# Cross-attention block on one core: the column sum of the context folded to 64 rows and taken in one product

## What is computed

```
g_x     = (g_w     @ x_2 + g_b).T          # 1024 x 256
theta_x = (theta_w @ x   + theta_b).T      # 1024 x 256
phi_x   =  phi_w   @ x_2 + phi_b           # 256 x 1024
W   = theta_x @ phi_x / 1024
y   = (W @ g_x).T                          # 256 x 1024
wy  = w_w @ y + w_b
out = bn_gamma * (wy - bn_mean) * rsqrt(bn_var + 1e-5) + bn_beta + x
```

## Time and profile before

| | |
|---|---|
| median of 3 runs | 783.51 us (783.49 to 783.71) |
| profiled execution, its own time | 783.43 us |
| its span, first to last instruction | 781.6 us |
| PE busy | 773.8 us (99% of the span) |
| POOL, DVE, ACT busy | 526.5, 495.3, 304.3 us |
| chain that ended last | PE 98%, DMA 1% |

### The profile page before, as it was taken

The page is one execution under the profiler, slowest core; times in us unless marked ns, Lnnn a source line. Parts: engine busy times, 40 slices in busy tenths (PEclk is TensorE's granted clock), DMA queues, the critical chain, the costliest instruction groups (busy, mean ns, idle before and its releaser), DMA issues.

```text
span 781.6 us, 11639 instructions
## 1 busy us (share of the span) xinstructions
PE 773.8 (99%) x4066; PEld 668.8 (86%) x4066; DVE 495.3 (63%) x891; ACT 304.3 (39%) x514; POOL 526.5 (67%) x358
## 2 busy tenths in 40 slices
PE   7999999999999999999999999999999999999998
PEld 6688888888888888888888888888888888888887
DVE  3874865749657385664848657396574847658255
ACT  5534533414344243543425345143542325334231
POOL 5939995757858477785758857478685767847500
DMA  9815573370835508264280734608365181740202
GB/s 278 202 67 130 194 188 135 79 245 1 215 107 110 212 22 216 84 161 161 54 252 17 188 134 90 232 0 215 107 132 190 33 229 59 173 150 1 108 1 107
DMA packets 55415, 103.17 MB, mean 132 GB/s; under 512 B 2506, under 2 KB 38244, under 8 KB 55396
## 3 DMA queue, kind: packets, MB, share of 16 engines
q1 hardware_dynamic: 53264, 101.86, 44.6%
q10 hardware_dynamic: 2132, 1.05, 0.6%
HBM read 69.35 MB, written 33.55 MB: 132 GB/s over the span
## 4 chain that ended last, share of the span: by engine, by line
PE 98%; DMA 1%; POOL 0%; DVE 0%; ACTq 0%; ACT 0%; issue 0%
PE wbank L699 58%; PE gbank L699 38%; PE wbank L871 1%; PE wbank L745 1%; DMA ctx_sb<-in_ctx_dram 1%; PE wbank L723 0%; PE wbank L751 0%; POOL ctxT_lo L303 0%; PE wbank L735 0%; DVE ctxT L504 0%; ACT ctxT_hi L357 0%; ACTq L368 0%; DVE x_sb L676 0%; ACTq L142 0%; PE wbank L710 0%
## 5 line engine op out<-in xcount | busy, mean ns | idle before, releaser
L303 POOL TENSOR_TENSOR ctxT_lo<-ctxT,ctxT_hi 128x512 fp32r<-128x512 f32 x124 | 168.0, 1356 | 202.9 <-ACT ctxT_hi L357 202.9
L314 POOL TENSOR_TENSOR ctx_sum<-ctx_sum,ctxT 128x512 f32<-128x512 f32 x108 | 157.8, 1461 | 0.2
L332 POOL TENSOR_TENSOR x_lo<-x_sb,x_hi 128x1024 fp32r<-128x1024 f32 x60 | 142.4, 2410 | 0.0
L357 ACT ACTIVATE mt<-wbank 128x512 fp32r<-128x512 f32 x64 | 37.9, 598 | 230.6 <-PE wbank L699 230.6
L689 DVE SCALAR_TENSOR_TENSOR x_sb<-wbank,const,x_sb 128x512 f32<-128x512 f32 x110 | 77.5, 746 | 69.4 <-PE wbank L699 69.3
L699 PE MATMUL wbank<-ctxT_lo,ctxT_hi 128*128 128x512 f32 x512 | 120.2, 390 | 0.5 <-POOL ctxT_lo L303 0.5
L357 ACT ACTIVATE ctxT_hi<-ctxT 128x512 fp32r<-128x512 f32 x124 | 76.6, 629 | 91.3 <-DVE ctxT L504 91.0
L534 DVE TENSOR_TENSOR stage<-gbank,mt 128x384 f32<-128x384 f32 x64 | 28.3, 485 | 131.7 <-PE gbank L699 131.7
L699 PEld LDWEIGHTS wbank<-ctxT_lo,ctxT_hi 128*128 128x128 f32 x512 | 94.6, 188 | 19.0 <-POOL ctxT_lo L303 0.7
L504 DVE STREAM_TRANSPOSE ctxT<-ctx_sb 128x512 f32<-128x512 f32 x124 | 78.8, 683 | 10.4 <-DMA ctx_sb<-in_ctx_dram 10.3
L699 PEld LDWEIGHTS gbank<-ctxT_hi 128*128 128x128 f32 x512 | 78.9, 189 | 4.0 <-issue 2.3
(11 more groups left out here) (113 smaller groups left out, 1334.4 us busy)
## 6 DMA issues: line engine op xcount, KB each, us to landing
x_sb<-in_x_dram SPq DMA_DIRECT2D x16, 2048.0 KB, 7.7
out_dram<-x_sb SPq DMA_DIRECT2D x63, 512.0 KB, 2.8
ctx_sb<-in_ctx_dram SPq DMA_DIRECT2D x60, 512.0 KB, 8.5
ctx_sb<-in_ctx_dram SPq DMA_DIRECT2D x4, 256.0 KB, 6.2
ctx_sb<-in_ctx_dram ACTq DMA_DIRECT2D x4, 256.0 KB, 7.0
x_sb<-in_L_xattn_w_w_dram SPq DMA_DIRECT2D x1, 512.0 KB, 9.0
stage<-in_L_xattn_theta_w_dram SPq DMA_DIRECT2D x1, 512.0 KB, 14.4
phi_nat<-in_L_xattn_phi_w_dram SPq DMA_DIRECT2D x1, 512.0 KB, 13.5
```

Of the source, the lines that this page charges most:

```text
L303: nc.gpsimd.tensor_tensor(ctxT_lo[:, c, :], turned_ctx(b, c), f(ctxT_hi[:, c, :]), ALU.subtract).then_inc(sem_, 1)
L314: nc.gpsimd.tensor_tensor(ctx_sum[:, :], ctx_sum[:, :], src, ALU.add).then_inc(ctxT_used, 1)
L332: nc.gpsimd.tensor_tensor(x_lo[:, k, :], x_sb[par][:, k, :], f(x_hi[:, k, :]), ALU.subtract).then_inc(x_lo_made, 1)
L357: nc.scalar.activation(dst, src, ACT.Copy).then_inc(sem_, 1)
```

## The change

The 128 rows of `ctx_sum` are folded to 64 before the split. ACT copies rows 64 to 127 to `fold` (`move_sum`); POOL adds them to rows 0 to 63, once rounded into `sum_parts` and once in full precision into `ctx_sum`, and subtracts the one from the other into `fold` (`sum_rest`); ACT rounds that into rows 64 to 127 of `sum_parts` (`pack_sum`). PE takes one product of ones with `sum_parts`. The rounded copy of the last add goes. The order on the engines changes too: on POOL `sum_rest` comes after `prep_x`; on ACT `move_sum` comes after `prep_x` and `pack_sum` at the start of the batch, ahead of the rows of M (in batch 0: after theta); in batch 0 on PE `column_sums` comes after two of the four blocks of t.

```diff
                 else:
                     pool.wait_ge(ctxT_used, CH * b + c)
-                    if c == CH - 1:
-                        nc.gpsimd.tensor_tensor(sum_hi[:, :], ctx_sum[:, :], src, ALU.add).then_inc(sum_split, 1)
                     nc.gpsimd.tensor_tensor(ctx_sum[:, :], ctx_sum[:, :], src, ALU.add).then_inc(ctxT_used, 1)
 
             def sum_rest(b):
                 pool.wait_ge(ctxT_used, CH * b + CH)
-                pool.wait_ge(sum_split, 2 * b + 1)
-                nc.gpsimd.tensor_tensor(sum_lo[:, :], ctx_sum[:, :], f(sum_hi[:, :]), ALU.subtract).then_inc(sum_split, 1)
+                pool.wait_ge(sum_moved, b + 1)
+                up = slice(0, P // 2)
+                nc.gpsimd.tensor_tensor(sum_parts[up, :], ctx_sum[up, :], fold[up, :], ALU.add).then_inc(sum_split, 1)
+                nc.gpsimd.tensor_tensor(ctx_sum[up, :], ctx_sum[up, :], fold[up, :], ALU.add).then_inc(sum_split, 1)
+                pool.wait_ge(sum_split, 3 * b + 2)
+                nc.gpsimd.tensor_tensor(fold[up, :], ctx_sum[up, :], f(sum_parts[up, :]),
+                                        ALU.subtract).then_inc(sum_split, 1)
 
             def prep_ctx(b):
-                pool.wait_ge(sum_split, 2 * b)
+                pool.wait_ge(sum_split, 3 * b)
...
-                sum_rest(b)
...
             def body(b, half, par, nxt, nxt2):
                 if nxt:
                     prep_ctx(b + 1)
                     prep_x(b + 1, 1 - par)
+                    sum_rest(b + 1)
...
+            def move_sum(b):
+                act.wait_ge(ctxT_used, CH * b + CH)
+                nc.scalar.activation(fold[0:P // 2, :], ctx_sum[P // 2:P, :], ACT.Copy).then_inc(sum_moved, 1)
+
+            def pack_sum(b):
+                act.wait_ge(sum_split, 3 * b + 3)
+                hi(sum_parts[P // 2:P, :], fold[0:P // 2, :], sum_packed)
...
                 if not first(b):
+                    pack_sum(b)
                     m_rows()
...
                 if nxt:
                     prep_x(b + 1, half + (1 if par else 0), 1 - par)
+                    move_sum(b + 1)
...
                 def column_sums():
-                    pe.wait_ge(sum_split, 2 * b + 2)
-                    mm(S_BANK[:, :], ones_r[:, :], sum_hi[:, :], True, False)
-                    mm(S_BANK[:, :], ones_r[:, :], sum_lo[:, :], False, True).then_inc(s_done, 1)
+                    pe.wait_ge(sum_packed, b + 1)
+                    mm(S_BANK[:, :], ones_r[:, :], sum_parts[:, :], True, True).then_inc(s_done, 1)
...
                 theta(0, (2, 3))
-                if first(b):
-                    pe.wait_ge(zb_taken, 1)
-                    column_sums()
                 pe.wait_ge(gram_lo_made, 3 * b + 3)
                 pe.wait_ge(low_lo_made, 2 * b + 1)
                 t_block(0)
                 t_block(1)
+                if first(b):
+                    pe.wait_ge(zb_taken, 1)
+                    column_sums()
```

More of the change, by code:

```diff
@@ L101, in xattn_kernel @@
         ctx_sum = sb("ctx_sum", [P, C])
-        sum_hi = sb("sum_hi", [P, C], F32R)
-        sum_lo = sb("sum_lo", [P, C], F32R)
+        fold = sb("fold", [P, C])
+        sum_parts = sb("sum_parts", [P, C], F32R)
         ident = sb("ident", [P, P])
@@ L196, in xattn_kernel @@
         ctxT_used = sem("ctxT_used")
-        sum_split = sem("sum_split")
+        sum_moved, sum_split, sum_packed = sem("sum_moved"), sem("sum_split"), sem("sum_packed")
         x_hi_made, x_lo_made = sem("x_hi_made"), sem("x_lo_made")
@@ L339, in _ @@
                 sum_up(0, c)
-            sum_rest(0)
             for k in (2, 3):
@@ L344, in _ @@
                                         ALU.subtract).then_inc(first_x_lo_pool, 1)
+            sum_rest(0)
             def body(b, half, par, nxt, nxt2):
@@ L421, in _ @@
                 z_hi_part(j)
+            move_sum(0)
             def body(b, half, par, nxt, nxt2):
@@ L461, in body @@
                 theta(0)
-                if not first(b):
+                if first(b):
+                    pack_sum(b)
+                else:
                     next_hi(4)
```

## The result

The changed kernel takes **792.1 us** (median of 5, 791.03 to 792.3), the kernel before in the same comparison 783.71 us: a ratio of 1.0105, 95% interval 1.009 to 1.012. It is slower, 8.4 us by the medians; the forecast was 791.2 with a range of 787.9 to 793.2. The profiled execution took 792.1 us, its span is 790.1 us against 781.6.

The account below looks back on a forecast made before the run. PE was taken to bound the kernel (98% of the last chain). Terms -3.4 + 0.3 + 9.4 + 1.4 = +7.7 on 783.43 gave 791.1, plus 0.08 for the median: 791.2 us, range 787.9 to 793.2.

Parts of the forecast that it names:

- The removed product: PE, batches 1 to 15: one 128x512 product fewer per batch, 15 x 0.227 = -3.4 us.
- POOL's fold in ordinary batches, hidden: Batches 2 to 15: three 64-row operations at 1.30 us; ACT's pack ends 1.2 us before M's first row, no cost.
- The rival at half the price: POOL's 64-row operations take half the time: 789.2 us, or 787.8 without the clock term; chance 0.12.
- The fourth row of M: Last three transposes wait for M's fourth row from ACT: 0.02 x 15 = +0.3 us, bounds 0 and 3.4.
- the handoff of 0.12: Time from ACT's finished fourth row of M to PE's weight load, 0.12 us, used to size that wait.
- Batch 0: Sum product moved behind two blocks of t; the fourth block, waiting for the bank, starts near 46.0: net +0.2 us.
- Batch 1's pause: ACT's wait for POOL's late fold holds the rows of M; PE idles some 9 us: +9.4 us, once.
- The clock: After batch 1's pause PE runs some products at the low clock: +1.4 us, bounds 0 and 2.8.
- The rival on the other side: No pause of PE in batch 1: -2.9 us, 780.6 us, faster than before; chance 0.06.

Follow-up runs that it names:

- experiment 4: Kernel before the change without the sum product of the low part, nothing added or moved; 780.19 us, ratio 0.9954.
- experiment 6: Changed kernel; from batch 1 on ACT packs after the high parts of S, PE takes the sum product behind the low bank's transposes; 783.61 us.
- experiment 3: Changed kernel with 32 products of 128x512 into an unused bank in PE's pause of batch 1; 789.94 us.
- experiment 1: Changed kernel with POOL folding batch 1's sum before the four x_lo instead of after them; 787.56 us, ratio 1.0036.
- experiment 2: Changed kernel with ACT packing the sum after the rows of M in batch 1 only; 788.22 us, ratio 1.0065.
- experiment 5: experiment 1 plus one wait: in batch 1 POOL begins the next context after DVE's three gram_lo; 781.31 us, ratio 0.9973.
- experiment 9: experiment 5 plus batch 1's pack between M's first two rows; in batch 0 pack before theta, sum product after one block of t; 780.68 us.

## Why the prediction was right

- **The removed product**: -3.4 forecast; the period fell by 0.219 us in 14 batches, and experiment 4 gave 3.5 us for 16. Right.
- **POOL's fold in ordinary batches, hidden**: forecast with 1.2 us of cover, measured 1.36. The price of a 64-row operation, taken at 1.30 between bounds of 0.65 and 1.64, is 1.25 to 1.30 where nothing else disturbs it: half the rows cost the same as all of them (1.28 for 128x512). The trace agrees with what the prediction took from the Trainium skill's GPSIMD Engine Reference (section 2, Architecture). The rival at half the price falls.
- **The fourth row of M**: forecast +0.3, measured at most 0.1 (14 times 0.227 less 0.219). In an ordinary batch the ten transposes take 1.06 us from their start to the next product (422.42 to 423.48), and 1.07 in the kernel before (412.49 to 413.56), so that the rows show no such wait with one product left. The step that was mis-sized is the handoff of 0.12 from the earlier trace rows; in experiment 6 it is 0.05. The mechanism is there, and decides as soon as the last product is moved too.
- **Batch 0**: forecast +0.2. PE's fourth block of t starts at 46.02, 0.22 after 45.80, but that agreement is luck: 0.18 was there before the first change of order (the last pair of theta stands at 40.76, before at 40.58, since the program's first load came later). From that pair to the fourth block it is 5.26 us against 5.22, so the change itself cost 0.04. The wait on the first block is there, but 0.26 us long (due at 45.76) where the forecast had 0.4.
- **Batch 1's pause**: forecast third part of M at 86.6, 9.4 later with the 0.2 of batch 0; measured 86.69, 9.3 us later than before. POOL's links came 0.2 to 0.3 late (x_lo to 81.55, fold to 85.36), as did M itself (74.09 in place of 73.78; in experiment 3, the same program up to there, it is 73.78 again, so this is scatter). ACT's pack took 0.65 to the next start, not 0.50, and the handoffs about 0.05, not 0.12, which cancel. Experiments 1, 2 and 3 tell the pause from its rivals.
- **The clock**: forecast +1.4, measured 2.4. This is the term that was mis-sized: I took the loss at the program's start, from one trace, for that of a pause. That loss itself is not fixed. Timelines of the 14 warm-up products in the kernel before and in experiment 6, and the granted clock of the kernel before in that stretch:

```profile
2.58 4.84 PE L699 MATMUL wbank<-x_hi,ones_r 128*128 128x512 f32 x14
...
2.58 6.21 PE L717 MATMUL wbank<-x_hi,ones_r 128*128 128x512 f32 x14
...
2.40:5.40 3.00, 2.99 (x8) 2.40 (x9) 1.33 (x8) 1.74 (x4) 0.00 (x0) 1.00 1.02 241
```

  The same products took 1.4 us more in one execution than in the other, so that the start could have cost 1.4 or 2.8. And the profile grants the full clock there (1.00): the rows show the slow pace at the start, not that it is the low clock; of the pause of batch 1 they show both. Its price varies as well: the five runs spread over 1.3 us (791.03 to 792.3), with a mean granted clock of 0.996 in the fastest and 0.994 in the others. By experiment 3 the 2.4 us behind the pause are wholly the clock.
- The difference between the medians was forecast at 7.7 and measured at 8.4: 1.0 more of the clock, less 0.2 of the fourth row and 0.1 of the pause. The other 0.2 of the 0.9 between 791.2 and 792.1 is that the kernel before stood at 783.71 in this comparison and not at 783.51.
- A slip in the range: its lower end, 787.9, leaves out the 787.8 that the rival at half the price gives without the clock term.

The rival on the other side (no pause, 780.6) was a true description of another kernel: experiment 5 (781.31) and 9 (780.68) are it.

## What to carry to other kernels

A change that is free in every ordinary iteration can be paid in the one where an engine still catches up after the prologue: look at the slack of each engine batch by batch, not at its share of the span. When a producer is moved behind other work, move the consumer's wait as well, and first see what stands behind that wait in its engine's list; here four rows of M stood behind a sum that was needed five microseconds later. And before a small piece of work is taken from the critical engine, see what it covers: the second of two may be worth less than the first.

## What was not expected of the hardware

- One DVE subtraction with both operands in SBUF lasted 11.50 us instead of 0.55, while POOL worked without a gap and at its own full speed. In ten of the eleven traces the first gram_lo of batch 1 begins while POOL is at work, and it ends 0.41 to 0.43 us after the end of a POOL operation. What differs is how many ends it lets pass. In the kernel before it began in the last x_lo (which ends at 83.99), lasted 0.75, and POOL's next operation was stretched to 1.64. In experiment 9 it began in the third x_lo and ended behind the fourth (at 85.94), in experiment 1 it ended only behind the eighth operation after that x_lo (at 95.09). The first gram_lo of the kernel before, and of experiment 9:

```profile
83.66 0.75 DVE L542 TENSOR_TENSOR gram_lo<-stage,gram_hi 128x384 fp32r<-128x384 f32 x1
...
83.36 3.00 DVE L568 TENSOR_TENSOR gram_lo<-stage,gram_hi 128x384 fp32r<-128x384 f32 x1
```

  So a start in the middle of an x_lo is not what decides; the kernel before has that too. Which of the two gives way, and why five runs of experiment 1 differ by 5 us, was not settled.
- Pauses of PE of 8.8, 7.9 and 4.75 us were followed by a granted clock of 0.50, and the work behind them lost 2.4, 2.0 and 2.2 us (the 2.0 from the 20 products from 97.18 to 101.59 in experiment 1, which take 2.39 us in experiment 5). A pause of 1.72 us in experiment 3 was followed by 1.00. Behind the one of 1.85 us at the start PE went on at the fast pace.
